# Decoder block, last feed-forward group: W3's tiles 2 and 3 one after the other, rows normalised and stored in three parts

## The reference

```python
x = _layernorm(x + attention(x))            # stabilised linear attention, 8 heads
x = _layernorm(x + experts(x, ctx, itok))   # 8 experts 256 -> 512 -> 256, gated
h = silu(x @ w1.T * s1) * (x @ w2.T * s2)   # 256 -> 1024
h = gelu(h @ h1.T * t1)                     # 1024 -> 1024
h = gelu(h @ h2.T * t2)                     # 1024 -> 1024
x = _layernorm(x + (h @ w3.T) * w3_s)       # 1024 -> 256; w3_s: one factor per column
# _layernorm: (x - mean) / sqrt(var + 1e-5) over the last axis
```

## Time and profile before

| | us |
|---|---|
| median of 3 runs | 833.45 |
| the runs | 833.44, 833.45, 836.83 |
| the profiled execution, its own time | 834.23 |
| its span in the trace | 832.4 |
| PE busy | 791.9 (95%) |
| PEld busy | 685.4 (82%) |
| DVE busy | 460.7 (55%) |
| ACT busy | 308.4 (37%) |
| POOL busy | 99.2 (12%) |
| DMA, mean over the span | 38 GB/s |

### The profile page before, as it was taken

One profiled execution on the slowest core, in us unless ns is written; L12 is line 12 of the kernel. 1 busy time (PEld: TensorE's weight loads), 2 busy tenths in 40 slices (PEclk: granted clock), 3 DMA queues, 4 the chain that ended last, 5 costly groups with the idle time before them and its releaser, 6 DMA issues.

```text
span 832.4 us, 12868 instructions
## 1 busy us (share of the span) xinstructions
PE 791.9 (95%) x4342; PEld 685.4 (82%) x4342; DVE 460.7 (55%) x1119; ACT 308.4 (37%) x552; POOL 99.2 (12%) x100
## 2 busy tenths in 40 slices
PE   5999849999999999999999989999999999999995
PEld 4888728888899998999899988888888888888884
DVE  4788657665577775777665655323632363245113
ACT  5677622222232313223232226342634354326331
POOL 2465520000220201102020000000000000000000
PEclk9999969999999999999999999999999999999998
DMA  8700000000311223131311000000000000000000
GB/s 265 254 0 2 0 2 2 0 2 26 102 51 41 90 57 94 51 101 38 95 46 51 26 10 1 1 0 1 25 0 0 0 25 0 0 7 19 1 1 26
DMA packets 16451, 31.46 MB, mean 38 GB/s; under 512 B 1680, under 2 KB 6160, under 8 KB 16400
## 3 DMA queue, kind: packets, MB, share of 16 engines
q1 hardware_dynamic: 16400, 30.82, 11.8%
HBM read 28.72 MB, written 2.10 MB: 37 GB/s over the span
## 4 chain that ended last, share of the span: by engine, by line
PE 44%; issue 44%; DVE 7%; ACT 2%; POOL 1%; DMA 1%; DVEq 0%; POOLq 0%; SPq 0%; ACTq 0%
PE bank L701 23%; PE bank L793 21%; DVE sp L954 1%; DMA wp_lo_f<-in_wproj 1%; DVE al L943 1%; DVE x_tok L1046 1%; DVE masked L919 1%; DVE vp L936 1%; DVE sgn L932 1%; POOL wx_lo_r L487 1%; DVE hx_lo L1069 1%; ACT sp L567 0%; ACT sp L574 0%; ACT hx_hi L614 0%; POOL rstd L514 0%
## 5 line engine op out<-in xcount | busy, mean ns | idle before, releaser
L614 ACT ACTIVATE hx_hi<-bank 128x512 fp32r<-128x512 f32 x128 | 76.7, 599 | 266.9 <-PE bank L701 266.8
L793 PE MATMUL bank<-wx_hi,hx_hi 128*128 128x256 f32 x512 | 144.8, 283 | 1.3 <-DVE x_tok L1076 0.9
L793 PE MATMUL bank<-wx_hi,hx_lo 128*128 128x256 f32 x512 | 144.9, 283 | 0.0
L793 PE MATMUL bank<-wx_lo_r,hx_hi 128*128 128x256 f32 x512 | 144.8, 283 | 0.0
L1069 DVE SCALAR_TENSOR_TENSOR hx_lo<-bank,hx_hi 128x512 fp32r<-128x512 f32 x128 | 88.0, 690 | 93.9 <-ACT hx_hi L614 90.3
L701 PE MATMUL bank<-xT_hi,wx_hi 128*128 128x512 f32 x256 | 103.5, 404 | 2.7 <-DVE hx_lo L1069 1.1
L793 PEld LDWEIGHTS bank<-wx_hi,hx_hi 128*128 128x128 f32 x512 | 97.8, 191 | 6.1 <-DVE x_tok L1076 1.1
L701 PE MATMUL bank<-xT_lo,wx_hi 128*128 128x512 f32 x256 | 102.0, 398 | 0.0
L793 PEld LDWEIGHTS bank<-wx_lo_r,hx_hi 128*128 128x128 f32 x512 | 97.8, 191 | 3.9
L701 PE MATMUL bank<-xT_hi,wx_lo_r 128*128 128x512 f32 x256 | 100.7, 393 | 0.0
L872 PE MATMUL bank<-ha_hi_r,wf_hi_r 128*128 128x512 f32 x256 | 100.0, 391 | 0.0
(11 more groups left out here) (140 smaller groups left out, 1326.1 us busy)
## 6 DMA issues: line engine op xcount, KB each, us to landing
stage<-in_wffn SPq DMA_DIRECT2D x44, 256.0 KB, 2.7
wx_lo_f<-in_wx SPq DMA_DIRECT2D x16, 512.0 KB, 4.6
xs_lo_f<-in_xT SPq DMA_DIRECT2D x4, 512.0 KB, 5.0
x_tok<-in_x SPq DMA_DIRECT2D x1, 2048.0 KB, 10.6
out<-x_tok SPq DMA_DIRECT2D x16, 128.0 KB, 1.7
wp_lo_f<-in_wproj SPq DMA_DIRECT2D x3, 512.0 KB, 6.8
ctx_sb<-in_ctx SPq DMA_DIRECT2D x4, 256.0 KB, 3.3
itok_sb<-in_itok SPq DMA_DIRECT2D x4, 256.0 KB, 4.3
```

The source lines that it names most:

```text
L614: act.activation(hx_hi[:, place, c], bank[b][:, :], ACT.Relu).then_inc(s_relu_ok, 1)
L793: mm = pe.matmul(bank[2 + j % 2][:, 0:D], x_, w_, start=(c == 0 and i == 0), stop=(c == XC - 1 and i == 2))
```

## The change

It touches four engines' programs for the last group (`last` true) and leaves the first three groups' work as it is.

- TensorE: the order of W3 in the last group becomes the pair (0, 1), then tile 2 alone (16 matmuls), then tile 3 alone (16 matmuls). The same matmuls are done.
- DVE: in the last group, tiles 0 and 1 are summed, their two means and variances formed; tile 2 is summed; tiles 0 and 1 are scaled; tile 2's mean and variance; tile 3 is summed; its mean and variance; tile 2 is scaled; tile 3 is scaled.
- POOL: in the last group three `pow` instructions, over columns 0:2, 2:3 and 3:4 of `rstd`, each with a semaphore value of its own.
- SP: the store loop covers 12 tiles; the last four stores are written out, with fixed addresses.

```diff
 # SP
-            with sp_.Fori(0, B) as t:
+            with sp_.Fori(0, B - J) as t:
                 sp_.wait_ge(s_e_xo, t + 1)
                 sp_.dma_start(out[bass.ds(t, 1)].rearrange("b t d -> t (b d)"), x_tok[:, bass.ds(t, 1)].rearrange("p o d -> p (o d)")
                               ).then_inc(s_out_done, 16)
+            for t in range(B - J, B):
+                sp_.wait_ge(s_e_xo, t + 1)
+                sp_.dma_start(out[t], x_tok[:, t]).then_inc(s_out_done, 16)
             sp_.wait_ge(s_out_done, 16 * B)
 # POOL
-            def ln_rstd(sem_in, sem_out, n):
+            def ln_rstd(sem_in, sem_out, n, a=slice(0, J)):
                 pool.wait_ge(sem_in, n)
-                pool.tensor_tensor(rstd[:, :], var_eps[:, :], neghalf[:, :], ALU.pow).then_inc(sem_out, 1)
+                pool.tensor_tensor(rstd[:, a], var_eps[:, a], neghalf[:, a], ALU.pow).then_inc(sem_out, 1)
...
-                ln_rstd(s_e_ve, s_e_rstd, g + 1)
+                for part in range(3 if last else 1):
+                    ln_rstd(s_e_ve, s_e_rstd, g + 1 + part, (slice(0, 2), slice(2, 3), slice(3, 4))[part] if last else slice(0, J))
 # TensorE
-                for pair in ((0, 1), (2, 3)):
+                for pair in ((0, 1), (2,), (3,)) if last else ((0, 1), (2, 3)):
 # DVE
-                for j in range(J):
+                def summed(j):
                     t = g * J + j
                     dve.wait_ge(s_e_y, t + 1)
...
-                norm_means(g * J, s_e_bn, s_e_mv, s_e_ve)
-                norm_apply(lambda j: group_row(g, j), lambda j: group_row(g, j), g, s_e_rstd, s_e_xo)
+                def means(part):
+                    for j in part:
+                        dve.wait_ge(s_e_bn, g * J + j + 1)
+                        dve.sem_inc(s_bn_tick, 1)
+                        dve.bn_aggr(mv[:, j], bn[:, j]).then_inc(s_e_mv, 1)
+                    dve.wait_ge(s_e_mv, g * J + part[-1] + 1)
+                    a = slice(part[0], part[-1] + 1)
+                    dve.tensor_scalar(var_eps[:, a], mv[:, a, 1], LN_EPS, None, ALU.add).then_inc(s_e_ve, 1)
+                def scaled(part, n):
+                    dve.wait_ge(s_e_rstd, n)
+                    for j in part:
+                        dve.tensor_scalar(group_row(g, j), group_row(g, j), mv[:, j, 0:1], rstd[:, j:j + 1], ALU.subtract, ALU.mult).then_inc(s_e_xo, 1)
+                if not last:
+                    for j in range(J):
+                        summed(j)
+                    means(range(J))
+                    scaled(range(J), g + 1)
+                else:
+                    summed(0)
+                    summed(1)
+                    means((0, 1))
+                    summed(2)
+                    scaled((0, 1), G)
+                    means((2,))
+                    summed(3)
+                    means((3,))
+                    scaled((2,), G + 1)
+                    scaled((3,), G + 2)
```

## The result

The changed kernel takes 832.96 us (median of 20 runs, 831.11 to 835.06), the kernel before 836.03 in the same number of runs (832.55 to 838.24). The ratio is 0.9963, 95% interval 0.9953 to 0.9973: about 3.1 us less (2.3 to 3.9). Timed a second time (s6) the ratio was 0.9972 (0.9954 to 0.9989), 2.3 us (0.9 to 3.8). Both intervals hold the 2.58 us that were forecast, and the gain stays under the 0.5% that was to count as a difference.

A forecast was written before the change was run, and what follows sets the result against it. PE's matmuls bound most of the span; only the last 9.6 us could change. Stores -2.64, register instructions -0.09, later variance +0.46 and shorter root -0.31 sum to -2.58 us, giving 830.9 us; range 830.1 to 833.0, the forecast's own 830.4 to 831.6.

The forecast's parts named there:

- The stores are late, not DVE: SP's queue at the end: stores 0.88 us apart while rows come every 0.32; removing three such distances saves 2.64 us.
- TensorE's edit costs nothing and starts tile 2 earlier by 0.54: W3 reordered in the last group: no added TensorE time, and DVE's sum of tile 2 starts 0.54 us earlier.
- The last variance comes 0.46 later: DVE's queue: two scalings and further means ahead of tile 3's sum end its var_eps 0.46 us later.
- The 0.13 for the extra semaphore instruction: Before tile 2's bn_aggr on DVE: possibly 0.13 us more delay if the added semaphore instruction isn't hidden.
- The last root, 0.70, between 0.38 and 1.01: POOL's final root over one column instead of four: 0.70 us instead of 1.01, saving 0.31 (0 to 0.63).
- Rival (a), POOL slowed by DVE: First root beside tile 2's multiply and add takes twice as long: gain 1.77, time 831.7 us; chance 0.10.
- Rival (b), instruction fetches: A 2.74 us fetch stall falls on DVE between tile 1's sum and the last scaling: 833.6 us; chance 0.06.
- Rival (c), stores that stay together: Last store waits for the one before, for example held 1.5 us on SP: 0.7 less gain, 831.6; chance 0.04.
- The sign "the last store still starts after 829": In the changed profile, a last store still starting after 829 us would mean the prediction fails outright; 827.7 was expected.
- The level: Absolute time: 834.23 us profiled less 2.58 makes 831.65, less 0.78 for the runs' median: 830.9 us.

The follow-up runs named there:

- s6: The changed kernel, unaltered, timed and traced again: ratio 0.9972 to the kernel before; tail (last group's first `y_s` to end of span) 11.02 us, 10.97 the first time.
- s1: The kernel before with only the last four stores written out with fixed addresses: ratio 1.0002; tail (last group's first `y_s` to end) 13.16 us against 13.67.
- s11: The changed kernel with tiles 0 and 1 scaled after tile 3's means: tail (last group's first `y_s` to end) 11.35 us against 10.97.
- s3: The changed kernel with W3 of the last group back in pairs (0, 1), (2, 3): tail (last group's first `y_s` to end) 11.58 us against 10.97.
- s7: The changed kernel with tile 2's scaling ahead of tile 3's means, so DVE idles during the last root: tail (first `y_s` to end) 11.10 us against 10.97.
- s5: The changed kernel with DVE's waits filled by tile 2's bn_aggr and var_eps and by moved scalings: ratio 0.9949 to the kernel before; tail 10.59 us against 10.97.
- s9: The changed kernel with DVE's waits filled and tile 2's store issued by ScalarE instead of SP: ratio 0.9964 to the kernel before; tail 10.38 us.
- s2: The changed kernel with all 16 stores back in the loop: tail (last group's first `y_s` to end) 11.23 us against 10.97.
- s10: The changed kernel with DVE's waits filled by other operations, the same kernel traced once more: tail 10.53 us, 10.59 the first time.
- s8: The kernel before with only fixed addresses for the last four stores, traced once more: tail (last group's first `y_s` to end) 13.16 us, as the first time.

## Why the prediction was right

The forecast's place and its size were right: nothing of the main stream changed, and the 2.58 us were 2.70. The time itself was inside the stated range by luck, as the last point says. Step by step:

- *The stores are late, not DVE.* Right, and the largest term. s1 separates its halves: of the 2.64, 1.27 can be had by fixed addresses alone, if the stores then land in 1.7 us, which they did not. Against s1 the change is 2.19 shorter: its last store starts 1.22 earlier and takes 2.07 to the end, not 3.0. That its stores lie apart is worth 0.38, net of what DVE gains by the other order (s11); the larger part is that rows are ready earlier.
- *TensorE's edit costs nothing and starts tile 2 earlier by 0.54.* Right: s3 gives 0.61 in the tail.
- *The last variance comes 0.46 later.* Measured 0.51, and the closeness is partly luck: an unrelated operation started 0.08, not 0.13, behind var_eps, twice, and the 0.2 us of idle time before the last var_eps was in no row of before. The 0.13 for the extra semaphore instruction did not come.
- *The last root, 0.70, between 0.38 and 1.01.* It was 0.64, of which 0.1 is the scaling beside it. With nothing beside it one column is 0.54 (s7) and four are 1.01; two took 0.69. That is some 0.38 fixed and 0.16 a column, where the lower end had 0.17 fixed and 0.21 a column, so the middle was a sound choice. For a root alone it was 0.16 too long; that the scaling gave 0.1 of it back is luck. I had put the first root at 1.01 although it has two columns; it made no difference, as DVE came later anyway.
- *Rival (a), POOL slowed by DVE.* Wrong in its place. The first root, beside tile 2's multiply and add, took 0.69, on the straight line from one column to four, and 0.70 in s3, where DVE stood still for more than half of it: not stretched. The one that was stretched ran beside a scaling, with one SBUF input. The rule of the Trainium skill (GPSIMD Engine Reference, 1. Specifications) names contention with VectorE instructions "in a 2-port perf mode or with two SBUF inputs"; the prediction used only the second half. That half does not show here: tile 2's root took 0.55 beside a multiply and an add, 0.54 alone. Whether the scaling falls under the first half no run shows; it takes 0.41 us, as long as the two-input add (0.42).
- *Rival (b), instruction fetches.* As priced, a stall of 2.7 us on DVE, it did not come. Whether it did in small is not shown: there are 0.2 us of idle time late in DVE's program, and in other kernels up to 0.5 us on a store's issue and 1.0 on its landing with a packet of instructions near by; the cause of each is open. In the change itself the one packet in the tail cost the stores nothing that can be seen.
- *Rival (c), stores that stay together.* Not in the change. In s5 it is what happened, at 0.90 us, with fixed addresses; it put the last store off by 0.5 (8.33, against 7.84 in s9).
- *The sign "the last store still starts after 829".* In the numbers of the trace it starts at 829.93, so as written the sign of failure came. It was given in the clock of one execution. Counted from the first `y_s` the limit is 829 - 818.73 = 10.27, and the store starts at 8.90 (8.97 were forecast).
- *The level.* Here the step "834.23 less 0.78" was weak. The three runs of before had a median of 833.45; twenty have 836.03. So 830.9 was 2.1 too low while the difference was right. The measured 832.96 lies outside the forecast's own range, 830.4 to 831.6, which had a chance of 0.72, and just inside the upper end of the whole range, 833.0. No rival and no term of the sum reaches beyond 831.7 on that side except (b); the 1.3 us up to 833.0 rest on one sentence on the run at 836.83, which gives no size. That they were enough is luck. That run said already that the spread is as large as the gain.

## What to carry to other kernels

The end of a program is a chain of its own: once the main engine has stopped, the last store's start decides, and a queue that needs 0.88 us for one store is late as soon as rows come faster; splitting the last group so that all stores but one are gone before the last row is ready took 2.4 us off here with the slow stores kept (s2), making the stores themselves faster 0.5 (s1), both together 2.7. Count the cost on the engine that orders the parts (0.5 us here), and let the producer finish the parts one by one as well (0.6 us). For a gain of this size measure from a point that the change can't move to the end of the span; span and single times varied by more than the gain.

## What the runs showed of the hardware that was not expected

- Stores of 128 KB 0.4 to 0.5 us apart are issued in 0.36 to 0.45 us each. One of them was held for 0.69 to 0.90 us at issue where it began together with a packet of instructions and 0.40 us behind another store (s5, s10, s11); with no store near, the same meeting cost nothing (s2). A store landed after 2.3 to 2.7 us instead of 1.7 where the packet began 0.8 to 1.2 us behind its start (s7, s1, s8). Each repeated kernel showed the same again; the causes are open.
- A root (`pow`) on POOL takes 0.54 us over 128 x 1, 0.69 over 128 x 2 and 1.01 over 128 x 4; a scaling of 128 x 256 with two per-partition operands takes it 1.23, against 0.41 on DVE.
- In five traces (the change, s2, s3, s6, s7) DVE stood idle for 0.2 us late in its program, before var_eps in four of them and before bn_aggr in s7; the cause is open.
- After TensorE's stop of 2.6 to 3.1 us at 493 to 500 us the granted clock fell to its lower level in nine of thirteen executions and not in the other four, with the same code. It cost 1.6 or 2.9 us up to the first `y_s` of the last group.
